# First cross attention of a two-layer perceiver block: TensorE takes its eight steps in twos

## What is computed

```python
q = (tgt @ Wq.T).reshape(b, t, H, HD)      # tgt = layernorm(x), H = 16 heads, HD = 16
k = (src @ Wk.T).reshape(b, s, H, HD)      # src = context, s = 4096
v = (src @ Wv.T).reshape(b, s, H, HD)
scores = einsum('bhtd,bhsd->bhts', q, k) / sqrt(HD)
attn = softmax(where(mask, scores, -inf), axis=-1)
out = einsum('bhts,bhsd->bhtd', attn, v)
```

## Time and profile before

| | us |
|---|---|
| median of three runs | 1784.96 |
| lowest and highest | 1783.38 to 1788.14 |
| the profiled execution | 1787.54 |
| its span, first to last instruction | 1785.7 |
| first to last scores matmul of this stage (L612) | 490.1 to 836.6 |

### The profile page before, as it was taken

One profiled execution on the slowest core, in us unless ns is written; L12 is line 12 of the kernel. 1 busy time (PEld: TensorE's weight loads), 2 busy tenths in 40 slices (PEclk: granted clock), 3 DMA queues, 4 the chain that ended last, 5 costly groups with the idle time before them and its releaser, 6 DMA issues. The chain is left out here.

```text
span 1785.7 us, 42086 instructions
## 1 busy us (share of the span) xinstructions
PE 1570.2 (88%) x15980; PEld 884.5 (50%) x15980; DVE 1148.1 (64%) x1735; ACT 874.5 (49%) x1176; POOL 683.7 (38%) x519
## 2 busy tenths in 40 slices
PE   3999999999499999999765967999999999977772
PEld 1455445545133333334342424777777777763442
DVE  4665665565599999995428647666666666515356
ACT  2555555555077777776240013555555555523430
POOL 2340000000111111111333006999999999943500
PEclk9999999999689999999887988999999999998886
DMA  4787888888432222220300037555555556112000
GB/s 163 198 213 231 210 237 223 223 223 195 139 94 67 64 66 68 64 64 17 153 1 1 1 88 224 140 154 152 153 153 153 153 142 161 28 34 90 1 1 12
DMA packets 178218, 212.19 MB, mean 119 GB/s; under 512 B 57096, under 2 KB 151572, under 8 KB 173486
## 3 DMA queue, kind: packets, MB, share of 16 engines
q1 hardware_dynamic: 177520, 210.45, 42.8%
q10 hardware_dynamic: 576, 0.00, 0.0%
HBM read 122.78 MB, written 87.57 MB: 118 GB/s over the span
## 5 line engine op out<-in xcount | busy, mean ns | idle before, releaser
L1121 POOL TENSOR_TENSOR x_r<-x_p 128x1024 f16<-128x1024 f32 x256 | 479.1, 1894 | 24.1 <-ACT x_p L1097 17.1
L1136 DVE TENSOR_REDUCE x_mx<-a_all 128x2 f32<-128x1024 f32 x249 | 304.9, 1224 | 147.2 <-PE a_all L1020 147.2
L1097 ACT ACTIVATE x_p<-s_all 128x1024 f32<-128x1024 f32 x256 | 248.4, 1022 | 223.2 <-PE s_all L1003 223.2
L702 ACT ACTIVATE x_p<-s_all 128x1024 f32<-128x1024 f32 x256 | 261.3, 1024 | 49.0 <-PE s_all L612 41.8
L757 DVE TENSOR_REDUCE x_mx<-a_all 128x1 f32<-128x512 f32 x352 | 229.4, 681 | 17.2 <-PE o_all L623 8.8
L1003 PE MATMUL s_all<-x_q,x_k 64*128 64x256 f16 x3072 | 210.2, 269 | 0.0
L1038 PEld LDWEIGHTS o_all<-x_v,x_p 128*128 128x128 bf16 x2048 | 178.8, 97 | 40.1 <-issue 40.1
L1038 PE MATMUL o_all<-x_v,x_p 128*128 128x129 f16 x2048 | 197.3, 221 | 0.9 <-POOL x_r L1121 0.9
L1039 PE MATMUL o_all<-x_v,x_r 128*128 128x65 f16 x2048 | 192.5, 193 | 0.0
L1039 PEld LDWEIGHTS o_all<-x_v,x_r 128*128 128x128 f16 x2048 | 180.7, 98 | 0.0
L1003 PEld LDWEIGHTS s_all<-x_q,x_k 64*128 64x128 f16 x3072 | 149.5, 94 | 62.2 <-issue 0.8
(11 more groups left out here) (345 smaller groups left out, 2803.4 us busy)
## 6 DMA issues: line engine op xcount, KB each, us to landing
values<-vst SPq DMA_DIRECT2D x16, 2064.0 KB, 10.4
x_v<-values SPq DMA_DIRECT2D x32, 1032.0 KB, 5.5
keys<-kst SPq DMA_DIRECT2D x32, 1024.0 KB, 6.7
x_k<-keys SPq DMA_DIRECT2D x128, 256.0 KB, 5.2
x_k<-keys SPq DMA_DIRECT2D x192, 64.0 KB, 2.1
values<-vst SPq DMA_DIRECT2D x16, 528.0 KB, 11.5
x_v<-values SPq DMA_DIRECT2D x32, 264.0 KB, 2.6
cf<-in_ctxT SPq DMA_DIRECT2D x16, 512.0 KB, 9.4
```

What stands on the lines that cost most here:

```text
L702: act.activation(prob[g % NP][:], chip.s_ps[g % 2][:].rearrange("p (c q) -> p c q", q=SQ), ACT.Exp, scale=hd ** -0.5).then_inc(p_ready, 1)
L1097: act.activation(prob[g % NP][:], chip.s_ps[g % 2][:].rearrange("p (c q) -> p c q", q=SQ), ACT.Exp, scale=hd ** -0.5).then_inc(p_ready, 1)
L1121: pool.tensor_tensor(rest[g % NP][:], prob[g % NP][:], hi, ALU.subtract).then_inc(rest_done, 1)
L1136: dve.tensor_reduce(mx[a[1] % 2][:, n // 4, 2 * (n % 4):2 * (n % 4) + 2], chunk_banks(u, g)[:, :].rearrange("p (h c) -> p h c", h=2), AX.X ...
```

## The change

PE works two steps at a time. In an even step it does the step's chunks and then the scores of two steps (g + 2 and g + 3). In an odd step it does the step's chunks and then the values of two steps. `VL` becomes 4, so four steps' values of a unit stand in the next unit, the last of them in step 3, where it was step 2. Within a step the chunks now come first.

The turned queries (`t`) go from place 8, ahead of step 4's chunks, to place 10 behind them. The folded output (`x`) goes from place 13, behind step 5's chunks, to place 15 ahead of step 7's. ACT copies `o` behind the exponential of step 5 instead of step 4, and the queries right behind that copy. The number of matmuls, reductions, exponentials and DMAs is the same.

```diff
-    GR, GK, W, VL, NP = 8, 4, 4, 3, 8
+    GR, GK, W, VL, NP = 8, 4, 4, 4, 8
...
-            place = [2 * g, 2 * g + 1, 2 * g + 2][0 if g < 4 else 1 if g < 6 else 2]
+            place = 2 * g + (g > 4) + (g > 6)
             pair = (ahead(u, 1), 6 + g) if g < 2 else (ahead(u, 2), g - 2)
             work = [(place + h, "c", pair[0], 2 * pair[1] + h) for h in range(2)]
             if g == 4:
-                work.insert(0, (8, "t", ahead(u, 1), 0))
-            if g == 5:
-                work.append((13, "x", ahead(u, -1), 0))
+                work.append((10, "t", ahead(u, 1), 0))
+            if g == 7:
+                work.insert(0, (15, "x", ahead(u, -1), 0))
...
                     for g in range(GR):
-                        if real(u) or (u[1] == -1 and g >= 6):
-                            s = u if g + 2 < GR else ahead(u, 1)
-                            if s:
-                                scores(s, (g + 2) % GR)
                         for place, kind, a, n in body_work(u, g):
                             wait_free(pe, u, place)
...
-                        if real(u):
-                            if g >= VL:
-                                values(u, g - VL)
-                            elif not is_first(u):
-                                values((u[0], u[1] - 1) if u[1] else (u[0] - 1, W - 1), GR + g - VL)
+                        s = u if g + 2 < GR else ahead(u, 1)
+                        if g % 2 == 0 and s and (real(u) or (u[1] == -1 and g == 6)):
+                            scores(s, (g + 2) % GR)
+                            scores(s, (g + 3) % GR)
+                        if g % 2 and real(u):
+                            for v in (g - 1 - VL, g - VL):
+                                if v >= 0:
+                                    values(u, v)
+                                elif not is_first(u):
+                                    values((u[0], u[1] - 1) if u[1] else (u[0] - 1, W - 1), GR + v)
...
-                        if g == 4 and ahead(u, -1):
+                        if g == 5 and ahead(u, -1):
                             copied(ahead(u, -1))
                         if g == 5 and ahead(u, 1):
-                            queries(ahead(u, 1), 8)
+                            queries(ahead(u, 1), 10)
```

More of the change, by code:

```diff
@@ L545, in chunks_before @@
         def chunks_before(u, place):
-            return nth(u, 16, 28 + (place if place < 8 else place - 1 if place < 13 else place - 2))
+            return nth(u, 16, 28 + place - (place > 10) - (place > 15))
         def wait_free(eng, u, place):
@@ L680, in _ @@
                 pe.wait_ge(x_done, UNITS - 1)
-                folded(None, 13, (PAIRS - 1, W - 1))
+                folded(None, 15, (PAIRS - 1, W - 1))
             @block.scalar
@@ L695, in body @@
                         if u[1] == -1:
-                            queries((0, 0), 8)
+                            queries((0, 0), 10)
                         return
@@ L785, in _ @@
                 all_units(dve, body)
-                output(13, (PAIRS - 1, W - 1))
+                output(15, (PAIRS - 1, W - 1))
                 dve.wait_ge(x_done, UNITS)
```

## The result

| us | before | after |
|---|---|---|
| median, lowest to highest, of four runs each | 1784.35, 1783.38 to 1788.14 | 1803.1, 1801.91 to 1805.58 |
| profiled execution, its span | 1787.54, 1785.7 | 1805.58, 1803.5 |
| first maximum (0) to the work behind the stage (L1201 before, L1203 after) | 355.68 | 372.18 |

The changed kernel takes 1.0103 times as long, 95% interval 1.0084 to 1.0121. The forecast was 1799.3 (1787 to 1811) and slower with a chance of 0.80.

The account below looks back on a forecast made before the run. DVE was taken to bound the stage: floor 10.34 plus holes 0.94 made a unit 11.28 us, +0.45. Over 29 units 13.0, plus 1.0 and 0.4 at start and end, gave 14.4: median 1799.3 us (1787 to 1811).

Parts of the forecast that it names:

- four durations of the hand-off: From a reduction over held chunk and two steps' values to the next reduction: 0.74 + 0.32 + 1.00 + 0.42 = 2.48 us.
- free switch: No cost of switching from values to chunk: 0.46 instead of 0.57, unit 10.94, kernel 1789.6 us.
- Step 3: Place 7 waits for place 4; DVE has four reductions, 2.39 us, against the hand-off: DVE idles (hole) 0.09.
- Step 5: Place 12 waits for place 9; turned queries hold place 10, so DVE has only 1.79 us of work: hole 0.69.
- Step 7: Place 17 waits for place 14; DVE has three reductions and the output, 2.35 us: hole 0.13.
- DVE's floor: DVE's own work in a unit: sixteen reductions (9.57), negated maximum 0.21 and output 0.56, together 10.34 us.
- One sign: If the forecast is right, DVE's total idle time on chunks rises from 6.4 us to over 20.
- Loads: Next unit's loads: their 1.2 us to spare shrinks to about 0; cost 0 to 0.3 a unit, taken as 0.
- Start and end: First unit's longer holes +0 to +3 us, taken +1; two more steps' values behind the last scores +0.4.
- The clock's: Rival: clock granted in half for a few units, 1808 us; chance 0.14 shared with loads and exponentials.
- The exponentials': Rival: ACT's exponentials bind in place of DVE, second scores wait, 1811 us; chance 0.14 shared with loads and clock.
- PE's saving feeds DVE: Rival, faster: PE's 1.0 us a unit saved in switches removes the 0.46 of holes, 1772 us; chance 0.09.

Follow-up runs that it names:

- spread kernel: Changed kernel with early loads, turned queries at place 9, output at 14, values spread over six steps, scores singly in steps 0 to 3: 1770.68 us.
- the first experiment: Changed kernel with a buffer's next loads released by the first of its unit's eight values instead of the eighth: median 1801.02 us, ratio 1.0099.

## Why the prediction came out

**Right, and for the reason given.** The four durations of the hand-off were all met: hold 0.74, values 0.32 behind, 1.00 for two steps' values, reduction 0.42 or 0.43 behind. Three had been read from single rows. The 1.00 was a sum (twelve passes less a length, plus a switch seen only in front of scores), taken over a free switch that would have given 0.46. With it three hand-offs of 2.48 or 2.49 stand in the unit shown, and the forecast was 2.48.

**Step 3**: hole forecast 0.09, found 0.09. **Step 5**: forecast 0.69, found 0.10 ahead of place 11 and 0.57 or 0.58 ahead of step 6's first reduction. The first part contradicts the sentence that the turned queries end before place 11 is late: from reduction 7 (661.15) over the turned queries (661.96), two steps' scores (662.28) and the chunk (662.73) to reduction 11 (663.15) it is 2.00, and DVE has only three reductions for it. It cost nothing, since both parts lie within one hand-off of 2.48. **Step 7**: forecast 0.13, found 0.26. Here the step that was wrong is the one on DVE's floor. The prediction took 0.56 for the output as DVE's own work. It is 0.41 or 0.42 in every kernel where the next chunk stands ready; 0.14 of it was a third hole of the kernel before. The floor is 10.2 and not 10.34. In the sum the two errors cancel, because that hole went from the output to step 7, and the unit came out at 11.30 to 11.40 for 11.28 plus the 0.11 of slower maxima that most units have. For the rivals it did not cancel: it made the possible gain look smaller than it is. The spread kernel took it.

One sign was missed: DVE's idle time on chunks was to go over 20 us and is 18.0. A wait counts only from the end of the reduction before, whose length of 0.68 overlaps the next one's start at 0.60, so it shows less than the holes do.

**Loads**: "about 0" of spare was right. The wait of the unit shown ends on the load, and PE's first chunk there started 1.26 behind the two steps' values (669.08) instead of 1.00. The price was the mis-sized term: taken as 0, it was 2.2 us by the first experiment, half of it in the last interval, whose first chunk waited 1.1 us:

```profile
830.70 0.37 PE L624 MATMUL a_all<-x_k,x_qa 64*128 64x512 f16 x1 [1.11 <-DMA x_v<-values]
```

It lay within the 9 us kept for the range. What the prediction did not do is add up the loads' round for itself, 2.84 + 5.81 + 2.68. It would have shown 11.3 as a second bound at the height of the first.

**Start and end**: +0.65 for +1.0, and +0.45 for +0.4. Another 0.8 us stood there before maximum 0, and 0.5 behind the stage, where nothing was changed. The clock, at 1.2 GHz in both at first, was granted in full from the window of 502 to 506 us on before (1.00), and one window later after (0.99), so part of the +0.65 is the clock's:

```profile
502.00:506.00 4.00, 4.00 (x29) 1.29 (x27) 2.58 (x4) 2.18 (x3) 0.00 (x0) 0.50 0.81 284
506.00:510.00 4.00, 3.87 (x48) 1.64 (x49) 3.52 (x6) 3.06 (x4) 0.00 (x0) 0.99 0.07 24
```

The forecast of 14.4 on the profiled execution stands against 18.0; on the median the measured time is 3.8 over the forecast. The hand-offs of 29 units took 13.2 (16.5 less 2.2, 0.65 and 0.45) for 13.0. The difference is the loads' 2.2, the 0.8 and 0.5 outside the stage, 0.2 outside the span and 0.2 in the hand-offs, less 0.3 at start and end.

**Rivals.** The clock's is out: 1.00 was granted from 510 us to the end of the stage, and PE idles at its chunks in every unit. The rule on short idles that make the clock fall (the Trainium skill, TensorE: Matmul & The Clock Gate, A second HAM failure mode: psum-queue depth-cycling) is not borne out by this stretch. The exponentials' is out for the changed kernel: from 520 to 820 us ACT waits for PE, 66.9 us, and PE never for ACT. That PE's saving feeds DVE was wrong in this change; the spread kernel, 15.6 us faster than before, shows that such a gain was there. The rule on the same gap coming back (the Trainium skill, Perfetto Trace Analysis, Identifying Performance Opportunities) agrees as far as it goes: the gaps end on chunks that a full bank held. But no bank was added to close them; over the same three banks, with early loads in both, the order of the work took the unit from 11.37 to 10.41.

## What to carry to other kernels

Where two engines pass few buffers back and forth, write down the chain from one release to the next: the held work, what is queued behind it, and the work that comes next. Compare it with what the consumer has to do meanwhile, at each place of the period. A longer block on the producer saved switches here and lengthened the chain. A buffer that holds something which the consumer does not work on leaves the consumer with less to do meanwhile, so it should not stand where the long block follows. Before a wait is moved, add up every cycle of waits that passes through it, loads too: their round (release, issue, landing, first use) is a bound of its own.

## What the runs showed of the hardware

- From the start of two steps of fp32 values (sixteen records) to the fp16 chunk behind them it is 1.00 us, from one step's (eight records) to fp16 scores 0.57: a step more costs 0.43, and the switch is the same.
- A chunk that waits for its bank starts 0.74 us behind the start of a reduction over 512 columns and 0.60 behind one over 384; a turned query 0.81 behind one over 512. Reductions over 384 columns come every 0.465 us, those over 512 every 0.60.
- From the start of the output's multiplication to the next reduction DVE needs 0.11 us when the chunk is there; the 0.25 of the kernel before held a wait.
- The part of the kernel behind this stage, the same in all, took 938.7 to 944.7 us. A difference of 3 us between two medians may lie there, and the stage's own ruler is sharper than the kernel's time.
